# A transformer block on one core: rotary work of the second batch moved to ScalarE and GpSimd, with five edits of order and placement

## What is computed

```python
Q, K, V = (x @ qw), (x @ kw), (x @ vw)          # reshaped to 16 heads of 8
Q, K = rope(Q, freq), rope(K, freq)             # x * cos + turned(x) * sin
score = einsum('bhqd,bhkd->bhqk', Q, K) / sqrt(8) - 1e10 * (1 - causal)
weights = softmax(score - max(score))
x = layernorm(x + merged(weights @ V) @ ow)
h = silu(x @ w1[e]) * (x @ w3[e])               # e = 0..3, 128 -> 512
x = layernorm(x + sum_e gates[:, e] * (h @ w2[e]))
```

## Time and profile before

| | us |
|---|---|
| median of 3 runs | 436.62 (435.84 to 437.49) |
| the profiled execution | 432.75 |
| its span, first to last instruction | 430.7 |
| TensorE busy in the span | 391.1 (91%) |
| VectorE busy | 315.1 (73%) |
| ScalarE busy | 265.1 (62%) |
| GpSimd busy | 193.5 (45%) |

### The profile page before, as it was taken

The page is one execution under the profiler, slowest core; times in us unless marked ns, Lnnn a source line. Parts: engine busy times, 40 slices in busy tenths (PEclk is TensorE's granted clock), DMA queues, the critical chain, the costliest instruction groups (busy, mean ns, idle before and its releaser), DMA issues.

```text
span 430.7 us, 7532 instructions
## 1 busy us (share of the span) xinstructions
PE 391.1 (91%) x2420; PEld 202.9 (47%) x2420; DVE 315.1 (73%) x1027; ACT 265.1 (62%) x377; POOL 193.5 (45%) x256
## 2 busy tenths in 40 slices
PE   4658769999999999999999888999999999999991
PEld 2243122232323323233232331788887887888770
DVE  3659888999999999999999543346576658656653
ACT  1233615687786867778687886566665656665550
POOL 7627611261343515235261322466565646655661
PEclk9959686999999999999999998999999999999996
DMA  6474841322213122131210000000000000000000
GB/s 216 153 203 91 286 115 23 75 53 57 52 22 89 39 70 51 25 93 22 74 35 3 1 3 2 0 2 1 2 1 24 2 1 24 2 1 3 24 0 24
DMA packets 45244, 21.13 MB, mean 49 GB/s; under 512 B 30995, under 2 KB 42899, under 8 KB 45206
## 3 DMA queue, kind: packets, MB, share of 16 engines
q1 hardware_dynamic: 44950, 20.47, 18.2%
q10 hardware_dynamic: 256, 0.20, 0.2%
HBM read 13.11 MB, written 7.35 MB: 47 GB/s over the span
## 4 chain that ended last, share of the span: by engine, by line
PE 70%; DVE 9%; ACT 5%; DMA 4%; issue 4%; POOL 3%; SPq 3%; ACTq 0%; POOLq 0%; DVEq 0%
PE o_bank L1127 14%; PE t_bank L1195 9%; PE bank L1084 9%; PE bank L1195 9%; PE t_bank L1206 9%; PE t_bank L1109 8%; PE small_bank L1084 5%; DMA q_op<-max_rows 3%; SPq L442 3%; ACT num L696 2%; DVE num L912 2%; POOL roped L509 1%; DVE num L985 1%; DVE x_w L850 1%; PE o_bank L1214 1%
## 5 line engine op out<-in xcount | busy, mean ns | idle before, releaser
L696 ACT ACTIVATE num<-t_bank 128x1024 f32<-128x1024 f32 (+2 forms) x160 | 142.8, 939 | 60.4 <-PE t_bank L1109 59.7
L610 POOL TENSOR_TENSOR hid_lo<-num,q_op 128x512 fp32r<-128x512 f32 x64 | 83.0, 1300 | 61.2 <-ACT q_op L749 60.0
L574 POOL TENSOR_SCALAR_AFFINE_SELECT num<-num 128x512 f32<-128x512 f32 x64 | 40.1, 636 | 120.7 <-ACT num L696 120.7
L1084 PE MATMUL bank<-k_op,q_op 128*128 128x512 bf16 (+7 forms) x256 | 71.8, 339 | 11.4 <-DMA q_op<-q_scratch 7.1
L1127 PE MATMUL o_bank<-num,v_op 128*32 128x512 f32 (+3 forms) x768 | 81.5, 503 | 0.1
L749 ACT ACTIVATE q_op<-num 128x512 fp32r<-128x512 f32 x64 | 40.5, 632 | 45.0 <-DVE num L985 44.5
L854 DVE TENSOR_REDUCE maxima<-bank 128x1 f32<-128x512 f32 x86 | 57.0, 684 | 2.6 <-PE bank L1084 1.6
L1109 PE MATMUL t_bank<-q_op,k_op 64*128 64x512 bf16 (+3 forms) x384 | 49.6, 337 | 4.3 <-ACTq L677 1.7
L1084 PEld LDWEIGHTS bank<-k_op,q_op 128*128 128x128 bf16 x256 | 21.2, 99 | 63.6 <-DVE maxima L854 23.4
L985 DVE TENSOR_TENSOR num<-bank,num 128x512 f32<-128x512 f32 x32 | 22.1, 691 | 30.7 <-ACT num L756 30.5
L850 DVE CUSTOM_DVE_ANT_0 mg_w<-bank,resid 128x256 f32<-128x256 f32 (+7 forms) x92 | 39.3, 447 | 4.7 <-PE bank L1084 3.8
(11 more groups left out here) (142 smaller groups left out, 629.2 us busy)
## 6 DMA issues: line engine op xcount, KB each, us to landing
q_op<-q_scratch SPq DMA_DIRECT2D x64, 48.0 KB
w_raw<-in_w_all SPq DMA_DIRECT2D x6, 512.0 KB, 4.0
k_op<-k_scratch SPq DMA_DIRECT2D x60, 48.0 KB, 1.9
xT<-in_x_feat SPq DMA_DIRECT2D x4, 256.0 KB, 5.9
q_op<-max_rows SPq DMA_DIRECT2D x64, 3.0 KB
out_tokens<-num SPq DMA_DIRECT2D x4, 256.0 KB, 2.3
q_scratch<-num SPq DMA_DIRECT2D x2, 384.0 KB, 2.8
k_scratch<-num SPq DMA_DIRECT2D x2, 384.0 KB, 2.8
```

Source lines behind the costliest of these rows:

```text
L574: pool.affine_select(out=tile, in_=tile, compare_op=ALU.is_ge, fill=0.0, base=0, pattern=[[0, GH], [1, P]], channel_multiplier=-1)\
L610: pool.tensor_tensor(hid_lo[:, m % HB, :], hid[:, m % HB, :], hid_hi[:, m % HB, :].bitcast(F32), ALU.subtract).then_inc(f_lo, 1)
L696: act.activation(num[:, t % PB, :, off:CH].rearrange("p (k i) t -> p i k t", i=2)[:, :, h:h + each, :], t_bank[k % TB][:, :, 0:each * (CH ...
L1084: ins = pe.matmul(ring(s, step)[:, i * width:(i + 1) * width], q_op[u][:, pr, j, :, :].rearrange("p i q -> p (i q)"), k_op[u][:, pr, lo:lo ...
```

## The change

Six edits, in the order of the program:

1. Cosine and sine of chunk 0 are loaded from ScalarE's queue, ahead of its first activation; those of chunk 1 follow the second chunk of x on SP's queue.
2. For blocks 0 and 1 the sum and the third part move from GpSimd to VectorE.
3. For blocks 4 to 7 ScalarE copies the two projections out of PSUM (`copy_turns`), GpSimd multiplies them with cosine and sine in place (`turn`) and also takes `first_rest`. VectorE has no rotary work in `PROLOGUE` any more. `PROJ_AT` and `T_AT`, `PV_AT` move: the first T step stands after 25 S steps, not 22. `FIRST` has an order of its own.
4. For chunk 0, four copies of `between` (r = 0, 1, 7, 8) move from ScalarE to VectorE and that of r = 9 to GpSimd. Units 0 and 1 of the experts stand before the last NORM of `LAST`.
5. In the expert loop `between` keeps its steps, but r = 1, 2, 3 come one unit later (`C_AT_UNIT`).
6. The w2 matmuls take the two products with `hid_hi` first and wait for `hid_lo` only ahead of the third.

```diff
-PROJ_AT = (12, 14, 16, 18, 20)
-T_AT, PV_AT = (22, 24, 25, 27, 28, 30), (29, 31, 33, 35)
+PROJ_AT = (12, 14, 17, 20, 23)
+T_AT, PV_AT = (25, 27, 28, 30, 31, 33), (34, 36, 37, 38)
...
-        plan.append(("NORM", NC - 1))
+        plan += [("E", 0), ("E", 1), ("NORM", NC - 1)]
...
+FIRST_ORDER = "ssssmssssnsssststsstsstsssttsspssttsspmsttssspssttsspssttsspssnttppp"
...
-FIRST = steady_plan(STEADY_ORDER.replace("t", "", SEG_T[0] - T_END[0]).replace("p", "", TI), done=TI - 1)
+FIRST = steady_plan(FIRST_ORDER, done=TI - 1)
...
+C_AT_UNIT = [0, C_STEPS, 1, 2, 3, *range(5, C_STEPS), C_STEPS]
...
-                if ch < NC:
-                    cols = slice(ch * CH, (ch + 1) * CH)
-                    sp.dma_start(cos_sb[:, cols], cos_t[:, cols]).then_inc(ld_tab[ch], 16)
-                    sp.dma_start(sin_sb[:, cols], sin_t[:, cols]).then_inc(ld_tab[ch], 16)
+                if ch == 1:
+                    load_table(sp, 1)
...
+            def first_rest(n):
+                pool.wait_ge(part_ready[0], n + 1)
+                pool.tensor_tensor(roped[:, n % 2, :], roped[:, n % 2, :], rope_part(n, 0), ALU.subtract)\
+                    .then_inc(rest_ready, 1)
+
+            def turn(n):
+                cols = slice(n // 2 % NC * CH, (n // 2 % NC + 1) * CH)
+                pool.wait_ge(turned, n + 1)
+                pool.tensor_tensor(by_cos[:, n % 2, :], by_cos[:, n % 2, :], cos_sb[:, cols], ALU.mult)\
+                    .then_inc(pool_turned, 1)
+                pool.tensor_tensor(by_sin[:, n % 2, :], by_sin[:, n % 2, :], sin_sb[:, cols], ALU.mult)\
+                    .then_inc(pool_turned, 1)
+                pool.wait_ge(pool_turned, 2 * (n - PROJ_FIRST + 1))
...
-            sum_of_turns(0)
-            sum_of_turns(1)
...
                     if step[0] == "P":
                         if step[1] < 2 * CHUNKS:
+                            turn(step[1])
                             sum_of_turns(step[1])
                         if step[1] > PROJ_FIRST:
                             third_part(step[1] - 1)
+                        if step[1] < 2 * CHUNKS:
+                            first_rest(step[1])
...
-            third_part(0)
-            third_part(1)
             for n in range(2, PROJ_FIRST):
                 sum_of_turns(n)
                 if n > 2:
...
+                if first and r == 9:
+                    pool.wait_ge(c_x1, 1 + ch + 1)
+                    pool.tensor_copy(x1[:, ch * TI:(ch + 1) * TI, :].rearrange("p i d -> p (i d)"), x1_w[:, :])\
+                        .then_inc(c_store, 1)
...
+            load_table(act, 0)
...
+            def copy_turns(n):
+                act.wait_ge(proj_ready, n + 1)
+                act.wait_ge(roped_ready, n - 1)
+                pair = 3 + 2 * (n % 2)
+                act.activation(by_cos[:, n % 2, :], bank[pair][:, :], ACT.Copy)
+                act.activation(by_sin[:, n % 2, :], bank[pair + 1][:, :], ACT.Copy).then_inc(turned, 1)
+
+            copy_turns(PROJ_FIRST)
+            copy_turns(PROJ_FIRST + 1)
             for n in range(PROJ_FIRST, 2 * CHUNKS):
                 first_part(n)
+                if n + 2 < 2 * CHUNKS:
+                    copy_turns(n + 2)
                 second_part(n)
...
-                    if step[0] == "C":
-                        between(0, 0, 0, step[1], first=True)
+                    if step[0] == "C" and step[1] == 12:
+                        between(0, 0, 0, step[1])
...
             turns_of(0)
-            for n in range(1, PROJ_FIRST):
+            sum_of_turns(0)
+            turns_of(1)
+            first_rest(0)
+            sum_of_turns(1)
+            third_part(0)
+            first_rest(1)
+            third_part(1)
+            for n in range(2, PROJ_FIRST):
                 turns_of(n)
-                first_rest(n - 1)
+                if n > 2:
+                    first_rest(n - 1)
             first_rest(PROJ_FIRST - 1)
...
-                    if step[0] == "P":
-                        if step[1] < 2 * CHUNKS:
-                            turns_of(step[1])
-                        if step[1] > PROJ_FIRST:
-                            first_rest(step[1] - 1)
...
+                if first and r == 0:
+                    dve.wait_ge(job_read, SB + LAST_JOBS)
+                    dve.wait_ge(c_mgt, 1 + ch)
+                    dve.tensor_copy(mg_w[:, :].rearrange("p (i g r) -> p i g r", i=TI, g=NG),
+                                    merged[:, 1:1 + NG, 0:TI, :].rearrange("p g i r -> p i g r")).then_inc(c_mg, 1)
+                if first and r == 1:
+                    dve.wait_ge(c_mgt, 1 + ch + 1)
+                    dve.wait_ge(c_y, 1 + ch)
+                    dve.tensor_copy(mg_t[:, :], turns[:, :]).then_inc(c_mgs, 1)
...
+                if first and r == 7:
+                    dve.wait_ge(c_x1t, 1 + ch + 1)
+                    dve.tensor_copy(x1_hi[ch], turns[:, :]).then_inc(c_hi, 1)
...
+                if first and r == 8:
+                    dve.wait_ge(c_log, 1 + ch)
+                    dve.wait_ge(c_lo, 1 + ch + 1)
+                    dve.tensor_copy(x1_tw[:, :], turns[:, :]).then_inc(c_x1s, 1)
...
+                    if step[0] == "E":
+                        if step[1] == 0:
+                            pe.wait_ge(c_top, 2)
+                            pe.sem_inc(f_w2, HB)
+                            pe.sem_inc(f_tr, 2)
+                        experts(0, step[1])
...
-                    pe.wait_ge(f_lo, ch * UNITS + m + 1 + HB)
+                    pe.wait_ge(f_hi, ch * UNITS + m + 1)
                     at = slice(2 * E * F + m * P, 2 * E * F + (m + 1) * P)
-                    for k, (ws, hs) in enumerate(((w_hi, hid_hi), (w_hi, hid_lo), (w_lo, hid_hi))):
+                    for k, (ws, hs) in enumerate(((w_hi, hid_hi), (w_lo, hid_hi), (w_hi, hid_lo))):
+                        if k == 2:
+                            pe.wait_ge(f_lo, ch * UNITS + m + 1 + HB)
                         ins = pe.matmul(bank[4 + e % 2][:, :], ws[:, at], hs[:, m % HB, :],
                                         start=f == 0 and k == 0, stop=f == FT - 1 and k == 2)
...
-            pe.wait_ge(c_top, 2)
-            pe.sem_inc(f_w2, HB)
-            pe.sem_inc(f_tr, 2)
-            for n in range(HEAD):
+            for n in range(2, HEAD):
                 experts(0, n)
...
-                    between(i + 1, n - HEAD)
+                    between(i + 1, C_AT_UNIT[n - HEAD])
```

More of the change, by code:

```diff
@@ L705, in stage, with between @@
                         act.activation(o_sb[c][:, :], o_bank[:, :], ACT.Copy).then_inc(o_copied, 1)
-                    if step[0] == "C":
-                        between(0, 0, 0, step[1], first=True)
+                    if step[0] == "C" and step[1] == 12:
+                        between(0, 0, 0, step[1])
             for n in range(-1, GROUPS - 1):
                 stage(STAGES[n + 1], n, split=n > 0)
-            def between(ch, b, c, r, first=False):
-                turns = bank[0] if first else bank[7]
+            def between(ch, b, c, r):
+                turns = bank[7]
                 if r == 0:
-                    act.wait_ge(job_read, SB + (LAST_JOBS if first else NJOBS))
+                    act.wait_ge(job_read, SB + NJOBS)
                     act.wait_ge(c_mgt, 1 + ch)
@@ L772, in _ @@
                         experts_hi(i + 1, n - UNITS)
-                    between(i + 1, (i + 1) // NC, (i + 1) % NC, n - HEAD)
+                    between(i + 1, (i + 1) // NC, (i + 1) % NC, C_AT_UNIT[n - HEAD])
                     experts_silu(i, n)
```

13 lines of the change are left out of this document (added).

## The result

| | us |
|---|---|
| after, median of 4 runs | 445.55 (444.72 to 447.68) |
| before, median of 4 runs on the same chip | 436.23 (434.77 to 437.49) |
| ratio | 1.022 (95% interval 1.017 to 1.027) |
| the profiled execution after, and its span | 444.72, 443.0 |

The kernel became 2.2% slower: 9.3 us by the medians. The two profiled executions differ by 12.3, since that of before was a short one (432.75).

The account below looks back on a forecast made before the run. The front's first T step was taken to wait for GpSimd's rotary chain, not VectorE. Terms: 11.0 - 2.0 - 2.5 - 1.1 - 0.5 = 4.9 us slower, so 441.5 us; range 436.5 to 446.5.

Parts of the forecast that it names:

- 11.0 was said for the front: Front, edit 3: GpSimd's chain delays the first T step to 60.3 us; the stage ends 11.0 us later (9.5 to 14).
- 1.26 and not 0.64 or 1.80: Front, blocks 4 to 7: a GpSimd product in place was priced at 1.26 us, between bounds of 0.64 and 1.80.
- r = 5 still has 2 us for GpSimd's power: 1.1 off: Expert part, edit 5: one unit later, TensorE's waits for `mg_t` go and r = 5 has time; 1.1 us faster (0 to 1.5).
- I take 2.0 off: Second stage: the new order of `FIRST` removes VectorE's idle time and spreads T steps; 2.0 us faster (0 to 3.0).
- 26 us long: Second stage: a sign that would show the forecast, the stage lasting 26 us where its window had been 28.0.
- -2.5 was said: Last stage, edit 4: the waits for `mg_w` and `x_tw` go, exponentials come earlier; 2.5 us faster (1.0 to 4.0).
- Gain about nothing: Last stage: units 0 and 1 ahead of NORM fill a 0.71 us wait, but VectorE's divisions wait for later transposes; about nothing gained.
- -0.54 against -0.5: Tail, edit 6: only one matmul instead of three remains after the wait for `hid_lo`; 0.5 us faster.
- The charge of 0.5 on the first x: Front, edit 1: tables ahead of x on a second queue share its DMA engines; 0.5 us charged (0 to 1.9).
- 0.2 net was said: Front, edits 1 and 2: first scores gain 0.7 us, less 0.5 charged; net gain 0.2 (-1.2 to +0.7).
- the 1.5 to 8 that had the chance of 0.58: Whole kernel: the forecast case, slower by 1.5 to 8 us, chance 0.58.
- rival (a): Front: GpSimd shares memory with VectorE for longer, chain operations cost 1.5 to 1.8 us; 3 to 4 more, 445 us; chance 0.15.

Follow-up runs that it names:

- E1: The changed kernel without edit 5 (r = 1, 2, 3 back at their units): 439.98 us, ratio 1.014 to the kernel before.
- E3: The changed kernel without edits 3 and 5, so edits 1, 2, 4, 6 and the order of `FIRST` remain: 429.24 us, ratio 0.990 to the kernel before.
- E4: The kernel before with edit 5 alone (r = 1, 2, 3 one unit later): 440.21 us, ratio 1.015.
- E10: E3 with the new P, T and PV places, plus an unread GpSimd sum beside the normalisation at r = 5: 432.15 us, ratio 0.996.
- E11: E3 with the new P, T, PV places and edit 5, GpSimd's rests beside the normalisation cut to 8 of 512 columns: 428.78 us, ratio 0.988.
- E8: E3 with the second stage's old order in place of the new `FIRST`: 430.52 us, ratio 0.992.
- E12: E9 without edit 1 (cosine and sine loaded by SP behind x, as before): 426.89 us, ratio 0.984.
- E9: E3 with the new P, T and PV places, and expert units 0 and 1 put back behind the last NORM: 428.60 us, ratio 0.987.

## Why the prediction was right or wrong

**Edit 3: right, in mechanism and size.** 11.0 was said for the front, 10.76 came; first T step at 59.59, said 60.3. The choice that mattered was 1.26 and not 0.64 or 1.80 for a product. E1 against E3 puts the edit at 10.7 by the medians as well. One reading behind it was loose without harm: the 0.69 of L810 was called "alone", but in the earlier trace rows it ran beside the sum that took 1.80.

**Edit 5: wrong in sign.** The step that failed is "r = 5 still has 2 us for GpSimd's power: 1.1 off". It asked when r = 5 could start, and took its own duration as given. The unit in which it now runs is the one where GpSimd works off two rests behind the power, and beside them the normalisation takes 2.94, not 1.11. TensorE then waits 1.8 at each of three boundaries. E4 shows the size (+5.9), E10 makes 3.4 of it out of one companion, E11 removes it by shortening the companions. The trace of before held the price. The layer norm at a chunk's end is four instructions of the same kind; beside two rests they took 2.8 us at three ends, and 1.11 at the last, where no rest was left:

```profile
L912 DVE TENSOR_SCALAR x_w<-resid,mv,rstd x16: 335/340/347, 252.3 to 376.4; 128x128 f32<-128x128 f32 x16
L912 DVE TENSOR_SCALAR num<-num,mv,rstd x16: 333/340/1325, 321.8 to 427.6; 128x128 f32<-128x128 f32 x16
...
321.52 2.53 POOL L610 TENSOR_TENSOR hid_lo<-num,q_op 128x512 fp32r<-128x512 f32 x2
...
321.82 2.83 DVE L912 TENSOR_SCALAR num<-num,mv,rstd 128x128 f32<-128x128 f32 x4
...
426.87 1.11 DVE L912 TENSOR_SCALAR num<-num,mv,rstd 128x128 f32<-128x128 f32 x4 [1.20 <-POOL rstd L614]
```

The wait for `mg_t`, for which the edit had 1.1 to win, went only from 1.1 to 0.8.

The Trainium skill (SBUF — State Buffer, section Who interferes with whom) states this as a rule: a `tensor_scalar` on SBUF can run in a mode that takes the ports shared with GpSimd, and whoever issues first holds them for the whole instruction, while the other "fully blocks". The trace agrees: the longest normalisation instructions took 1.30 to 1.33, and a rest 1.29. By that rule the new place of r = 5 was to be priced at up to two rests more. I had asked about sharing only for edit 3.

**The second stage: the size was wrong.** The 2.0 were taken from a window of 28.0 us against 25.4 for an equal stage. But I had cut that window by eye, from 60.5 to 88.5; from join to join the stage took 26.21, and an equal one 25.84. There was 0.4 to win by that measure. So "I take 2.0 off" is the second step that failed; -0.18 came, though the stage was "26 us long" as forecast. E8 gives the new order 0.8 against E3 at the same clock, the stage of before gives it nothing (26.21 against E3's 26.19), and E12's stage was another 1.3 shorter than E9's, at the higher clock.

**Edit 4: right, with one term missed.** -2.95 came, -2.5 was said. Underneath, the copies and the clock gave 3.5 (E9 against before: 27.20 against 30.74), near the upper bound of 4.0 since the half clock did not recur, and units 0 and 1 ahead of NORM took back 0.8. "Gain about nothing" is the step that failed there; the reason for a loss stood behind it in the same sentence, the divisions that wait for transposes twelve matmuls further back.

**Edit 6: right**, -0.54 against -0.5. **Edits 1 and 2: not resolved.** The charge of 0.5 on the first x was 0.76 in the profile (6.65 against 5.89). The first scores came 0.9 earlier all the same (24.14 against 25.07), where 0.2 net was said. But one trace does not settle this: in the ten other kernels with both edits the first scores came between 23.89 and 25.42, in E4, whose front is that of before, at 25.28.

**The sum** was 4.9, and 12.3 came in the profiled executions. The failed steps are 6.6 and 1.8 of that difference of 7.4, the others -1.0 together. The forecast of 441.5 still lay only 4 below the measured median, in part by luck, because the profiled execution of before was 3.5 below its median and that of after only 0.8. The measured 9.3 us lie inside the stated range, but above the 1.5 to 8 that had the chance of 0.58. They are nearest to rival (a)'s 445, whose mechanism did not occur at the front, where it was placed: GpSimd meeting VectorE cost the time, but in the expert part, and there VectorE was the one that lost. Two things stay open: why before's median moved between sessions (436.2 beside the changed kernel, 433.6 to 434.4 in the others), and why the parts multiply to 1.030 by the medians (0.990 for E3, 1.025 and 1.015 for edits 3 and 5 upon it) where the whole measured 1.022 (1.017 to 1.027).

## What to carry to other kernels

When an instruction is moved in time, look at what the other engine that shares its memory does in the new place, and price the instruction beside that, not at its old duration; the maximum in the view by line shows whether such a price occurs anywhere. Measure a stage from one event to the same event of the next stage, not by a window cut to round numbers. When a single stage is compared, look at several traces of the same stage: the first scores and the second stage moved by over 1 us here between kernels that do not differ there. An engine with slack over the whole span can still be the bound for 24 us, if the work moved to it is a chain with one reader at its end.
